# Attention kernel: projection, transpose of the maxima and pieces of the maxima at other places of a step

## What is computed

```python
q = (x @ Wq).reshape(b, n, HEADS, DIM_HEAD).transpose(0, 2, 1, 3)
k = (context @ Wk).reshape(b, m, HEADS, DIM_HEAD).transpose(0, 2, 1, 3)
v = (context @ Wv).reshape(b, m, HEADS, DIM_HEAD).transpose(0, 2, 1, 3)
scores = jnp.einsum('bhnd,bhmd->bhnm', q, k) * scale
attn = jax.nn.softmax(scores, axis=-1)
out = jnp.einsum('bhnm,bhmd->bhnd', attn, v)
out = out.transpose(0, 2, 1, 3).reshape(b, n, HIDDEN)
return out @ Wo + bo
```

## Time and profile before

| quantity | value |
|---|---|
| median of three runs | 941.9 us |
| the profiled execution | 938.92 us, of which its span 937.1 us |
| TensorE matmuls busy | 891.1 us, 95% of the span |
| VectorE, ScalarE, GpSimd busy | 551.5, 351.8 and 593.3 us |
| attention, from the first transpose to the last output | 108.1 to about 658 us |
| mean granted clock of TensorE in 108 to 658 us | 0.99 |

### The profile page before, as it was taken

The page is one execution under the profiler, slowest core; times in us unless marked ns, Lnnn a source line. Parts: engine busy times, 40 slices in busy tenths (PEclk is TensorE's granted clock), DMA queues, the critical chain, the costliest instruction groups (busy, mean ns, idle before and its releaser), DMA issues. The chain is left out here.

```text
span 937.1 us, 12963 instructions
## 1 busy us (share of the span) xinstructions
PE 891.1 (95%) x4616; PEld 527.6 (56%) x4616; DVE 551.5 (59%) x1123; ACT 351.8 (38%) x493; POOL 593.3 (63%) x397
## 2 busy tenths in 40 slices
PE   6998799999999999999999999998899999989993
PEld 3655355545555555565554564544678888855551
DVE  2898557667747767757766756754645121145552
ACT  2245144434525544435443434451441121123332
POOL 0454198898878889869889869882114400047785
PEclk9999899999999999999999999999999999999997
DMA  8013300000001000001000001040795100423210
GB/s 277 27 50 111 109 1 1 23 1 1 1 1 45 24 1 1 1 1 46 23 1 0 2 1 45 1 157 1 197 351 193 54 14 22 135 90 111 81 39 15
DMA packets 42873, 52.86 MB, mean 56 GB/s; under 512 B 4400, under 2 KB 33856, under 8 KB 42816
## 3 DMA queue, kind: packets, MB, share of 16 engines
q1 hardware_dynamic: 35808, 44.21, 14.8%
q0 software_dynamic: 3744, 6.32, 2.1%
q10 hardware_dynamic: 3264, 1.57, 0.6%
HBM read 38.42 MB, written 17.59 MB: 60 GB/s over the span
## 5 line engine op out<-in xcount | busy, mean ns | idle before, releaser
L607 POOL TENSOR_TENSOR accG<-accG,probs 128x1024 f32<-128x1024 f32 (+1 forms) x170 | 405.2, 2384 | 38.5 <-ACT probs L630 23.4
L630 ACT ACTIVATE probs<-st 128x1024 f32<-128x1024 f32 (+1 forms) x208 | 212.7, 1026 | 202.9 <-PE st L794 197.3
L674 DVE TENSOR_REDUCE mxp<-mx 128x1 f32<-128x512 f32 x360 | 231.9, 686 | 60.0 <-PE mx L780 54.6
L816 PE MATMUL av<-probs,V 128*64 128x512 f32 (+1 forms) x832 | 191.7, 598 | 0.0
L780 PE MATMUL mx<-K_hi,Q_hi 64*128 64x512 f32 (+1 forms) x480 | 137.9, 380 | 0.0
L816 PEld LDWEIGHTS av<-probs,V 128*64 128x64 f32 (+1 forms) x832 | 55.4, 136 | 105.7 <-issue 83.9
L794 PE MATMUL st<-Q_hi,K_hi 64*128 64x512 f32 (+1 forms) x416 | 113.0, 445 | 0.9 <-ACT probs L630 0.9
L780 PEld LDWEIGHTS mx<-K_hi,Q_hi 64*128 64x128 f32 x480 | 73.8, 184 | 52.0 <-issue 26.8
L794 PE MATMUL st<-M,ones_r 64*128 64x512 f32 (+1 forms) x416 | 101.1, 392 | 0.0
L794 PE MATMUL st<-Q_hi,K_lo 64*128 64x512 f32 (+1 forms) x416 | 96.7, 392 | 0.0
L794 PE MATMUL st<-Q_lo,K_hi 64*128 64x512 f32 (+1 forms) x416 | 94.5, 394 | 0.0
(11 more groups left out here) (198 smaller groups left out, 1238.0 us busy)
## 6 DMA issues: line engine op xcount, KB each, us to landing
w_gate_up<-in_gate_up SPq DMA_DIRECT2D x4, 2048.0 KB, 20.1
w_down<-in_down SPq DMA_DIRECT2D x2, 2048.0 KB, 15.8
xs<-scratch_sorted_x SPq DMA_DIRECT2D x31, 128.5 KB
scratch_sorted_x<-zero SPq DMA_DIRECT2D x7, 514.0 KB, 8.3
xT<-in_xT SPq DMA_DIRECT2D x4, 512.0 KB, 6.7
xring<-in_x SPq DMA_DIRECT2D x4, 512.0 KB, 8.7
scratch_x1b<-xT SPq DMA_DIRECT2D x4, 512.0 KB, 2.9
x<-scratch_x1b SPq DMA_DIRECT2D x4, 512.0 KB, 4.3
```

The lines of the kernel that those rows point to most:

```text
L607: pool.tensor_tensor(total[0:r], so_far[0:r], probs[0:r, place(S, t)], ALU.add).then_inc(g_add, 1)
L630: act.activation(probs[0:r, place(S, t)], st[g % 2][0:r, :], ACT.Exp, scale=DH ** -0.5).then_inc(a_probs, 1)
L674: dve.tensor_reduce(mxp[:, F % 2, h * QT + i, j:j + 1], mx[h][:, 0:kn], AX.X, ALU.max).then_inc(v_mx, 1)
L816: mm = pe.matmul(av[h * DH:(h + 1) * DH, :], V[0:r, t, (2 * p + h) * DH:(2 * p + h + 1) * DH], probs[0:r, place(S, t), h * QC:(h + 1) * QC ...
```

## The change

A step of TensorE now is: tiles with pieces in all 13, the sums behind the first run as before, and behind the last run the projection of the queries of step S + 2, the transpose of the maxima of S + 1, both halves of the output (in the first step of a chunk), and then the last values. The late pair between values is gone; tile 0 carries a pair, and tile 4 carries both pieces in slot 4. The banks of the two output halves are swapped. ScalarE and VectorE follow: the high part of S + 2 stands behind the last exponential, the copy of `av` behind it; the low part and `M` stand behind the last maximum, and the statistics in front of a step's pieces. The divisions come behind pieces 10 and 18, not 8 and 16.

```diff
-PIECE_AT = {1: (0, 1), 2: (1, 2), 3: (2, 3), 4: (3, 4), 5: (0, 1), 6: (1, 2), 7: (2, 3), 8: (3, 4),
+PIECE_AT = {0: (0, 1), 1: (1, 2), 2: (2, 3), 3: (3, 4), 4: (4, 4), 5: (0, 1), 6: (1, 2), 7: (2, 3), 8: (3, 4),
             9: (0, 1), 10: (0, 1), 11: (1, 2), 12: (2, 3)}
-SHORT = 8
-LATE_PAIR = 10
-DIVIDE_AFTER = (8, 8, 16, 16)
+SHORT = 9
+DIVIDE_AFTER = (10, 10, 18, 18)
...
+            q_high(1)
             for S in range(STEPS):
                 c, p = divmod(S, PAIRS)
-                if S > 0:
-                    copy_av(S - 1)
-                if S + 1 < STEPS:
-                    q_high(S + 1)
                 for t in range(KT):
                     exp(S, t)
                     if p == 1 and t == NORM_AFTER and c > 0:
                         norm(c - 1)
-            copy_av(STEPS - 1)
+                if S + 2 < STEPS:
+                    q_high(S + 2)
+                copy_av(S)
...
-            for S in range(STEPS):
+            max_rows(0)
+            q_low(1)
+            for S in range(STEPS - 1):
                 c, p = divmod(S, PAIRS)
-                max_rows(S)
                 if p == 1 and c > 0:
                     statistics(c - 1)
-                if S + 1 < STEPS:
-                    q_low(S + 1)
...
+                all_maxima(S + 1)
+                if S + 2 < STEPS:
+                    q_low(S + 2)
+                max_rows(S + 1)
+                if p == 0 and c > 0:
+                    for i in range(QT):
+                        residual(c - 1, i, (mx[0], misc)[i // 2])
...
+                if n == 2:
+                    pe.wait_ge(v_mT, F)
...
                 if half == 0:
                     pe.wait_ge(d_wo, 16)
                     pe.wait_ge(v_o, (c + 1) * PAIRS * DIVS)
+                    pe.wait_ge(v_mx, ((c + 1) * PAIRS + 1) * PIECES)
                 else:
-                    pe.wait_ge(v_mx, ((c + 1) * PAIRS + 1) * PIECES)
-                bank = (misc, mx[0])[half]
+                    pe.wait_ge(v_lo, (c + 1) * PAIRS + 2)
+                bank = (mx[0], misc)[half]
...
             pe.wait_ge(g_ones, 4)
+            max_transpose(0)
+            q_proj(1)
             for S in range(STEPS):
                 c, p = divmod(S, PAIRS)
                 ahead = S + 1 < STEPS
-                max_transpose(S)
-                if ahead:
-                    q_proj(S + 1)
                 n = 1
                 for run, given in zip(RUNS, VALUES):
                     for t in run:
-                        tile(S, t, n if ahead and t in PIECE_AT else None)
-                        n += 2 if t in PIECE_AT else 0
+                        tile(S, t, n if ahead else None)
+                        n += 2
                     if run is RUNS[0] and S > 0:
                         sums(S - 1)
-                    if run is RUNS[-1] and p == 0 and c > 0:
-                        output(c - 1, 0)
+                    if run is RUNS[-1]:
+                        if S + 2 < STEPS:
+                            q_proj(S + 2)
+                        if ahead:
+                            max_transpose(S + 1)
+                        if p == 0 and c > 0:
+                            output(c - 1, 0)
+                            output(c - 1, 1)
                     for t in given:
-                        if t == LATE_PAIR and ahead:
-                            piece(S + 1, n)
-                            piece(S + 1, n + 1)
                         values(S, t)
-                if p == 0 and c > 0:
-                    output(c - 1, 1)
```

More of the change, by code:

```diff
@@ L709, in _ @@
             dve.wait_ge(v_mask, 1)
-            for S in range(STEPS):
+            max_rows(0)
+            q_low(1)
+            for S in range(STEPS - 1):
                 c, p = divmod(S, PAIRS)
-                max_rows(S)
                 if p == 1 and c > 0:
                     statistics(c - 1)
-                if S + 1 < STEPS:
-                    q_low(S + 1)
[L717 to L725, removed]
-                    if p == 0 and c > 0:
-                        residual(c - 1, 2, mx[0])
-                        residual(c - 1, 3, mx[0])
+                for n in range(1, PIECES + 1):
+                    piece_maximum(S + 1, n)
+                    for i, at in enumerate(DIVIDE_AFTER):
+                        if n == at and S > 0:
+                            divide(S - 1, i)
+                all_maxima(S + 1)
[5 more added lines that the diff above has]
+                        residual(c - 1, i, (mx[0], misc)[i // 2])
             for i in range(DIVS):
@@ L753, in q_proj @@
                 at_least(pe, v_o, (F - 2) * DIVS)
-                if pair == 2 and c > 0:
-                    pe.wait_ge(v_r, (c - 1) * QT + 2)
                 if F == 1:
```

## The result

| | before | after |
|---|---|---|
| median of 20 runs each | 941.18 us | 943.59 us |
| profiled execution's span | 937.1 us | 940.0 us |
| ratio after to before | | 1.0029, 95% interval 1.0019 to 1.0038 |
| predicted | | 943.1 us (936.4 to 947.2) |

The change makes the kernel slower by 0.3%, 2.7 us by the ratio. Twenty runs on each side resolve it; the prediction had called anything within 0.5% no change.

A forecast was written before the change was run, and what follows sets the result against it. TensorE's instruction sequence was taken as the bound, issuing nearly all of each 32.22 us step. Terms -8.8 + 9.6 + 0.6 - 0.45 + 0.2 = +1.2 us, added to the 941.9 median, gave 943.1 us (range 936.4 to 947.2).

The forecast's parts named there:

- Term 1: From a step's last tile to the next first tile: 5.50 us instead of 6.14, 14 x -0.63 = -8.8 us.
- Rival 2: End of 14 steps: values wait for the transpose's whole result, 0.29 us more each, 947.2 us; chance 0.08.
- Rival 3: Step's end: every change between rows, columns and whole array costs 0.38 us in full, giving 935.3 us; chance 0.03.
- Term 2: First run of tiles: 6.93 us against 6.29, the tenth piece waiting for the eighth maximum; 15 steps, +9.6 us.
- Rival 1: Fifth tile of the first run: its piece does not wait, costing 15 x 0.22 = 3.3, so 936.8 us; chance 0.14.
- Rival 4: Whole step: the moves do nothing, pieces being bound by VectorE; a step keeps 32.2 us, 941.9 us; no chance given.
- The smaller terms: Attention's start +0.6 us once, steps behind an output 3 x -0.15 = -0.45 us, last step with pieces +0.2 us.
- What covers what: Step's end: the projection's 1.8 us cover the maxima; high part, low part, mask product and GpSimd's additions cost nothing.

The follow-up runs named there:

- halved maxima: The changed kernel with the maxima of pieces 7 and 8 taken over half of their columns only; ratio 0.9953 to the kernel before.
- earlier places: The changed kernel with the pieces of tiles 2, 3 and 4, in the first run, in earlier slots; ratio 0.9956 to the kernel before.
- moves alone: The changed kernel with pieces in tiles 1 to 12 as before and the thirteenth pair behind tile 12, before the projection; ratio 1.0112 to the kernel before.
- pieces alone: The kernel before with pieces in tiles 0 to 12, no late pair, divisions behind pieces 10 and 18, nothing else moved; ratio 1.0177 to the kernel before.
- transpose first: The changed kernel with transpose and projection exchanged behind the last tile; ratio 1.0172 to the kernel before.
- both with earlier places: Two versions of the changed kernel: pieces in earlier slots in the first run only (ratio 0.9956), or in the last run too (ratio 0.9903).

## Why the prediction was right, and where it was off

**Term 1, the end of a step: expected 5.50 us, measured 5.61.** The four values took 3.59 (3.58 expected), projection with the change into it 1.82 (1.81). The transpose was mis-sized: 0.20, not 0.11. Rows of the changed kernel's output step tell the cause:

```profile
272.15 0.27 PE L746 MATMUL mx<-ident,nm 128*128 128x128 f32 x1
272.26 3.62 PE L845 MATMUL mx<-wo,oT 128*128 128x256 f32 x16
275.71 3.62 PE L845 MATMUL misc<-wo,oT 128*128 128x256 f32 x16
279.26 3.66 PE L813 MATMUL av<-probs,V 128*64 128x512 f32 x16
```

Behind a matmul on the whole array, the transpose takes 0.11 where another such matmul follows, and 0.20 where values follow. Sixteen passes take 3.45 before passes of their own kind and 3.55 before values. So the change of the array's use in front of values costs 0.1 us, as I had read it from the earlier trace rows; my mistake was to count it inside the block of values. It falls on what stands in front of the block, and the block, measured from its own first start, is 3.59 behind the transpose and behind the projection alike. Term 1 is then 14 x -0.53 = -7.4 us, not -8.8.

Rival 2 (0.29 more for the transpose) does not appear. Rival 3 does not appear at its price of 0.38 a change, but that price was a misreading: it set the 0.59 us of a pass of 512 columns against the 0.21 us between passes of 256 columns. Like against like, a matmul outlasts the start of its successor by 0.16: 0.59 against 0.43 in the projection, 0.27 against 0.11 in the transpose in front of the output. The rows at the changes come out at just that wait. The transpose ends at 207.72 (207.45 + 0.27); the first pair of values is listed at 207.65, but lasts 0.65 instead of 0.59, as its weight load was late, so its own work begins at about 207.71. The last values end at 211.31, and the first piece of the next tile, listed at 211.24, lasts 0.50 instead of 0.39. So at these changes nothing starts before the end of the matmul in front, where it elsewhere starts 0.16 before it; in the listed start times this costs the 0.1 us. The trace therefore agrees with the Trainium skill ("TensorEngine Tiling (Array Packing)", Key Properties), that changing the tiling mode drains TensorE, as far as ends that the profile models can show it.

**Term 2, the first run: expected 6.93 us, measured 6.95,** with the wait at the place and for the maximum that was named. Of the 0.66 us above the run before, the halved maxima and the earlier places show that the wait is 0.43, and the moves alone that the rest (0.23) is the pair. 15 x 0.66 = +9.9 us, against +9.6. Rival 1 needed no wait here, and is refuted. Rival 4, that the moves change nothing, is right for the step as a whole by accident only: its end did get 0.53 us shorter, and the moves alone and the pieces alone each cost time.

**The smaller terms.** The last step with pieces waits as foreseen:

```profile
615.49 0.33 PE L746 MATMUL mx<-ident,nm 128*128 128x128 f32 x1 [0.89 <-DVE nm L676]
```

At the start the first tile now follows its high part by 0.65 us where it stood 0.11 ahead of it: 0.76, as expected. But the part itself came 0.4 sooner. The four passes of the first projection, from 111.0 on in both, lasted 3.37 us here and 3.78 in the kernel before: the granted clock is 0.50 of full speed (1.2 GHz) until about 113.8 here and until 115.0 there, and 1.00 (2.4 GHz) after. That is a difference of two executions, not shown to be one of the kernels. The rows of the changed kernel:

```profile
114.41 0.60 ACT L613 ACTIVATE Q_hi<-misc 128x512 fp32r<-128x512 f32 x1 [11.18 <-PE misc L756]
...
115.06 0.50 PE L777 MATMUL mx<-K_hi,Q_hi 64*128 64x512 f32 x1 [0.69 <-ACT Q_hi L613]
```

The steps with an output gained more than expected. From the last tile to the sums they take 19.48 us (270.33 to 289.81 in the changed kernel) against 19.78 (268.87 to 288.65), while a plain step lost 0.15 there (12.56 against 12.41): 0.45 us each. Of this I had 0.15, for the statistics, which measure 0.2: the first run behind an output was 6.48 us against 6.29 of a plain step, and is now 6.96 against 6.95. The rest stands at the step's end: the two halves of the output take 3.45 + 3.55 us together where they took 3.65 + 3.56 apart. I had called their cost unchanged, but standing together they have two changes of the array's use less. No run isolates this.

**What covers what** held: the low part and the product with the mask made no tile wait, GpSimd's last addition ended at 213.84 (204.05 + 9.79), 4.3 us before the sums, and the transpose waited for nothing except in the last step. Exchanging it with the projection showed that the maxima need 0.9 of the 1.8 us of cover.

**The sum.** I had +1.2 us. In the trace the sums of the last step come 1.7 us later (651.82 against 650.12), and 1.2 more is lost behind them. There the last output waits for VectorE, and the granted clock is at its lower level, 1.2 GHz, for longer in the changed kernel's execution:

```profile
656.00:666.50 10.50, 7.21 (x28) 5.00 (x28) 8.09 (x27) 4.35 (x12) 2.60 (x9) 0.84 0.43 112
```

```profile
656.00:667.00 11.00, 8.47 (x23) 5.28 (x24) 8.76 (x25) 2.98 (x9) 0.82 (x4) 0.53 0.37 103
```

The first line is the kernel before, the second the changed one; the column before the last two is the clock, 0.84 against 0.53 of full speed. In the kernel before, the clock falls at about 661.1, after idle times of TensorE of 1.39, three times 0.50 and 1.13 us and within one of 1.51; in the changed one at about 656.5, after 1.39 and 0.50.

The traces of the experiments settle part of the cause. From the sums of the last step to the first matmul of the gate in the mixture of experts (L1280 of the kernel before), the same work in all, it is 12.13 us in the changed kernel and in four experiments built on it (halved maxima, transpose first, and both with earlier places). It is 11.32 in the kernel before, in the pieces alone and in the moves alone, where the clock is at full speed almost up to there (kernel before) or beyond. But it is 11.81 in the kernel before with earlier places in its last run, whose clock is 0.55 from 652 to 663: the early fall comes with the old order too, and it is absent in the moves alone, which have the new one. So the low level is worth up to 0.8 of the 1.2 us and differs between executions; that the change makes it more frequent is not shown.

By its parts attention is now -7.4 (14 steps' ends) + 9.9 (15 first runs) - 1.35 (three output steps) + 0.3 (start, with the earlier clock) + 0.2 (last step with pieces) = +1.65 us, which is the 1.7 in the trace. Against my +1.2, the end of a step cost 1.4 us more, mostly by the transpose's place, the first runs 0.3 more, and the output steps and the start gave 1.2 back. The two terms that decide were right in mechanism, but the closeness of the total (943.1 against 943.59) is partly luck: these errors cancel, and the base of 941.9, a median of three runs, lay 0.7 us above the 941.18 of twenty. The measured change is 2.7 us (interval 1.8 to 3.6), so about 1 us of it lies outside the terms of the sum.

## What to carry to other kernels

When a producer and a consumer alternate over banks that must be freed, look at the idle time of the slower one early in the run, not only at the wait at its end: here 0.36 and 0.33 us of VectorE's idle time turned into 0.43 us of TensorE's, and moving pieces of three tiles by one or two slots gave it back. A table that paces work for n pairs has to be paced anew when a pair is added. Price a wait by where it stands and what stands behind it: 60 waits before and 60 after, less in sum (15.3 against 19.6 us), and still 6.5 us more of the span.

## What the runs showed that was not expected

A change between using the whole of the array and its columns costs about 0.1 us in start times at the places measured (0.20 against 0.11 for the transpose, 3.55 against 3.45 for sixteen passes), and the matmul behind it begins where the one in front ends by the profile, 0.16 us after its successor would have begun otherwise. The kernel before had a curable wait of its own, worth 0.4% of the time with one line of a table (0.9957), and with that wait and the new one of the first run cured the change gains where it had lost.
